# Attention before a gated layer: one transposing transfer per half tile, two V projections moved forward, weighted values in two halves

## What is computed

```
qkv = (x @ Wqkv).reshape(b, l, 3, H, DH)          # H = 16 heads of DH = 16
q = q * cos + rotate_half(q) * sin ; k likewise
scores = einsum('bqhd,bkhd->bhqk', q, k) * DH ** -0.5
out = einsum('bhqk,bkhd->bqhd', softmax(scores), v)
```

## Time and profile before

| | |
|---|---|
| median of 3 runs | 1267.89 us (1267.33 to 1268.97) |
| profiled execution | 1267.04 us, its span 1265.2 us |
| attention stage | from 0 to about 546 us |
| TensorE busy | 1175.9 us (93%) |
| VectorE busy | 944.3 us (75%) |
| ScalarE busy | 897.1 us (71%) |
| GpSimd busy | 580.8 us (46%) |
| DMA moved | 194.50 MB, mean 154 GB/s |

### The profile page before, as it was taken

How to read it: one execution, slowest core, us unless ns; L and a number is a source line. 1 busy time by engine, 2 the same in 40 slices (tenths; PEclk the granted TensorE clock), 3 DMA queues, 4 the chain that set the end, 5 groups by cost and what they waited for, 6 DMA issues and landing times. The chain is left out here.

```text
span 1265.2 us, 25878 instructions
## 1 busy us (share of the span) xinstructions
PE 1175.9 (93%) x8369; PEld 863.4 (68%) x8416; DVE 944.3 (75%) x1865; ACT 897.1 (71%) x1979; POOL 580.8 (46%) x593
## 2 busy tenths in 40 slices
PE   3699999999999999879999969999999999999997
PEld 2233333333333333258899969999999999999897
DVE  4588878778888888559666657777777777777586
ACT  5277877777777776757655457777777777777686
POOL 6232323232323210026377735666666666666763
PEclk8599999999999999999799989999999999999999
DMA  6735655564644451042032267677777776776463
GB/s 152 129 72 148 131 146 127 138 129 92 138 86 100 83 115 35 18 159 68 1 132 92 98 194 246 235 256 255 236 234 240 255 249 236 234 247 204 140 196 103
DMA packets 260826, 194.50 MB, mean 154 GB/s; under 512 B 152272, under 2 KB 243664, under 8 KB 260752
## 3 DMA queue, kind: packets, MB, share of 16 engines
q1 hardware_dynamic: 253936, 174.82, 49.0%
q0 software_dynamic: 6816, 18.75, 4.1%
HBM read 122.06 MB, written 37.52 MB: 126 GB/s over the span
## 5 line engine op out<-in xcount | busy, mean ns | idle before, releaser
L554 DVE TENSOR_REDUCE att_mx<-att_psA 128x1 f32<-128x512 f32 x512 | 330.2, 681 | 90.3 <-PE att_psA L357 89.9
L462 ACT ACTIVATE att_prob<-att_psB 128x512 f32<-128x512 f32 x512 | 289.4, 604 | 116.0 <-PE att_psB L367 101.3
L357 PE MATMUL att_psA<-att_qk 96*128 96x512 bf16 x512 | 198.9, 393 | 17.2 <-DVE att_mx L554 7.2
L1642 ACT ACTIVATE exp_psU<-exp_psU,ew_b 128x256 f32<-128x256 f32 x312 | 126.9, 446 | 102.6 <-PE exp_psU L1599 102.6
L367 PE MATMUL att_psB<-att_qk 128*128 128x512 bf16 x465 | 176.8, 383 | 9.6 <-DMA att_qk<-att_mrow 8.2
L1693 DVE CAST exp_hh<-exp_psU 128x512 fp32r<-128x512 f32 x156 | 107.8, 691 | 102.8 <-ACT exp_psU L1642 102.8
L1582 PE MATMUL exp_psD<-exp_w2h,exp_hh 128*128 128x256 f32 x624 | 175.7, 282 | 0.0
L1597 PE MATMUL exp_psU<-exp_xh,exp_w1h 128*128 128x256 f32 x624 | 173.5, 278 | 1.4 <-DVE exp_xl L1684 1.4
L1599 PE MATMUL exp_psU<-exp_xh,exp_w1l 128*128 128x256 f32 x624 | 173.0, 277 | 0.0
L1598 PE MATMUL exp_psU<-exp_xl,exp_w1h 128*128 128x256 f32 x624 | 173.0, 277 | 0.0
L1583 PE MATMUL exp_psD<-exp_w2l,exp_hh 128*128 128x256 f32 x624 | 172.4, 276 | 0.0
(11 more groups left out here) (228 smaller groups left out, 2860.4 us busy)
## 6 DMA issues: line engine op xcount, KB each, us to landing
ew_w<-ew SPq DMA_DIRECT2D x40, 1024.0 KB, 5.7
exp_w<-ew SPq DMA_DIRECT2D x38, 1024.0 KB, 6.3
slots_x<-pre_acc SPq DMA_DIRECT2D x13, 780.0 KB, 4.7
pre_spare<-slots_x SPq DMA_DIRECT2D x39, 260.0 KB, 4.1
out_g<-rows_y SPq DMA_DIRECT2D x32, 256.0 KB, 3.8
ew_b<-eb SPq DMA_DIRECT2D x39, 128.0 KB
pre_spare<-xT SPq DMA_DIRECT2D x8, 512.0 KB, 5.2
attn_rows<-att_ob SPq DMA_DIRECT2D x8, 512.0 KB, 2.8
```

What stands on the lines that cost most here:

```text
L357: pe.matmul(psA[A_BANK[n % U]][:, :], r[:, 0, qt * P:(qt + 1) * P], r[:, 1, :], start=True, stop=True).then_inc(s_amm, 1)
L462: act.activation(prob[:, n % PR, :], psB[B_BANK[n % U]][:, :], ACT.Exp, scale=SCALE).then_inc(s_exp, 1)
L554: dve.reduce_max(mx[:, g % 2, n % U:n % U + 1], psA[A_BANK[n % U]][:, :], AX_X).then_inc(s_max, 1)
```

## The change

- The stack of a tile is laid out by head, q and k side by side (`[P, 2, H, 2, P]`), and so is `qk`. One transposing transfer takes both of a half tile; it waits for both. Semaphore counts go from 32 to 16 a tile. The rotation's and the pieces' access patterns follow.
- V of tiles 2 and 3 (`LATE_ASIDE`) is projected at the end of period -3 into psB[2] and psV, before the scores begin. The waits on psX no longer ask for V in periods up to 0; instead the first row score waits for 2 copies of V, the first column score for 3.
- Weighted values are added in two halves of the 512 queries, at units 2 and 3 of each four. The output copy goes from unit 3 to 4, its turn from 6 to 5.
- The maxima are turned by four matmuls, one for each row tile, into 12 x 512 rather than by one into 48 x 128; they are copied at unit 10 instead of 11, and a transfer reads 4 rows of 512 instead of 16 of 128.
- The second repeat of pieces goes from units 10, 11 to 11, 12; the slots are zeroed with at most one transfer a period, over more periods.

```diff
+    LATE_ASIDE = (2, 3)
-    PROJECT_QK, ROPE, COPY_OUT, TURN_OUT, NORM_OUT = 0, (1, 2, 2), 3, 6, (6, 7)
-    PROJECT_V, COPY_V, SPLIT_MAX, TURN_MAX, COPY_MAX = 13, 13, 8, 10, 11
-    PIECE_1, SPREAD_1, PIECE_2, SPREAD_2, SPLIT_X = 6, (7, 8), 9, (10, 11), 0
+    PROJECT_QK, ROPE, COPY_OUT, TURN_OUT, NORM_OUT = 0, (1, 2, 2), 4, 5, (6, 7)
+    PROJECT_V, COPY_V, SPLIT_MAX, TURN_MAX, COPY_MAX = 13, 13, 8, 10, 10
+    PIECE_1, SPREAD_1, PIECE_2, SPREAD_2, SPLIT_X = 6, (7, 8), 9, (11, 12), 0
-    ADD_PV = 2
+    ADD_PV = (2, 3)
...
-        stack = a.sb("stack", [P, 2, 2, H, P], BF16)
-        qk = a.sb("qk", [P, 2, 2, H, L], BF16)
+        stack = a.sb("stack", [P, 2, H, 2, P], BF16)
+        qk = a.sb("qk", [P, 2, H, 2, L], BF16)
-        mstk = a.sb("mstk", [P, PIECES, U], BF16)
-        mrow = a.sb("mrow", [PIECES * U, 2, P], BF16)
+        mstk = a.sb("mstk", [P, PIECES, G, NT], BF16)
+        mrow = a.sb("mrow", [PIECES * G, 2, L], BF16)
-        ASIDE_QK, ASIDE_V = {1: psA[0], 2: psB[0], 3: psB[1]}, {0: psA[1], 1: psA[2]}
+        ASIDE_QK, ASIDE_V = {1: psA[0], 2: psB[0], 3: psB[1]}, {0: psA[1], 1: psA[2], 2: psB[2], 3: psV}
...
-            CLEAR = [p for p in range(NG) for _ in range((1, 1, 2, 0)[p % NT])][1:CHUNKS + 1]
+            CLEAR = [p for p in range(1, NG) if p % NT < NT - 1][:CHUNKS]
...
-                    sp.dma_start(qk[96 + k:97 + k, g // HG % 2, 0, heads(g), :].rearrange("o j (t c) -> o (j t) c", c=P),
-                                 mrow[k * U:(k + 1) * U, g % 2, :]).then_inc(s_mld[g % 2], 16)
+                    sp.dma_start(qk[96 + k:97 + k, g // HG % 2, heads(g), 0, :], mrow[k * G:(k + 1) * G, g % 2, :]).then_inc(s_mld[g % 2], 16)
...
-                for i, ready in enumerate((s_p3, s_qsp)):
-                    sp.wait_ge(s_stk, 2 * tile + 2)
-                    sp.wait_ge(ready, tile + 1)
-                    sp.dma_start_transpose(qk[:, b % 2, i, some, t * P:(t + 1) * P],
-                                           stack_of(tile)[:, i, some, :].rearrange("p h c -> p (h c)")).then_inc(s_tr[half][tile % 2], 16)
+                sp.wait_ge(s_stk, 2 * tile + 2)
+                sp.wait_ge(s_p3, tile + 1)
+                sp.wait_ge(s_qsp, tile + 1)
+                sp.dma_start_transpose(qk[:, b % 2, some, :, t * P:(t + 1) * P].rearrange("p h i c -> p (h i) c"),
+                                       stack_of(tile)[:, some, :, :].rearrange("p h i c -> p (h i c)")).then_inc(s_tr[half][tile % 2], 16)
...
                 if n == 0:
                     pe.wait_ge(s_init, SET_UP)
+                    pe.wait_ge(s_vev, 2)
...
+                if n == 0:
+                    pe.wait_ge(s_vev, 3)
...
-                for s, n in ((s_vev, p + V_LEAD), (s_qrd, p + QK_LEAD + (use > QK)),
+                for s, n in ((s_vev, p + V_LEAD if p > 0 else 0), (s_qrd, p + QK_LEAD + (use > QK)),
...
-                pe.matmul(psX[0:PIECES * U, 0:P], mstk[:, :, :].rearrange("p m u -> p (m u)"), ident[:, :], start=True, stop=True).then_inc(s_mtr, 1)
+                for t in range(NT):
+                    ins = pe.matmul(psX[0:PIECES * G, t * P:(t + 1) * P], mstk[:, :, :, t], ident[:, :], start=True, stop=True)
+                ins.then_inc(s_mtr, 1)
...
-                    m = pe.matmul(psV[32 * j:32 * j + 32, :], V[:, b % 2, kt, hg * G + j, :], prob[:, (n + j) % PR, :],
-                                  start=(kt == 0), stop=(kt == NT - 1))
-                m.then_inc(s_pv, 1)
+                    m = pe.matmul(psV[32 * j:32 * j + 32, some], V[:, b % 2, kt, hg * G + j, :], prob[:, (n + j) % PR, some],
+                                  start=(kt == 0 and part == 0), stop=(kt == NT - 1), skip_group_check=True)
+                if part == 1:
+                    m.then_inc(s_pv, 1)
...
-                    if u % G == ADD_PV and valid(n - ADD_PV - G, NG * U):
-                        add_pv((n - ADD_PV - G) // U, ((n - ADD_PV - G) % U) // G)
+                    for part in range(2):
+                        first = n - ADD_PV[part] - G
+                        if u % G == ADD_PV[part] and valid(first, NG * U):
+                            add_pv(first // U, first % U // G, part)
...
-                    if u == PROJECT_V and valid(p + V_LEAD, NT * B):
+                    if u == PROJECT_V and valid(p + V_LEAD, NT * B) and p + V_LEAD not in LATE_ASIDE:
                         project(p + V_LEAD, True)
+                if p + QK_LEAD == FILL - 1:
+                    for tile in LATE_ASIDE:
+                        project(tile, True)
```

More of the change, by code:

```diff
@@ L186, in heads_of, with by_kind @@
         def heads_of(t):
-            return t[:, :].rearrange("p (h d) -> p h d", d=DH)
+            return t[:, :].rearrange("p (h i d) -> p h i d", i=2, d=DH)
+        def by_kind(t):
+            return t[:, :].rearrange("p (h i d) -> p i h d", i=2, d=DH)
         def stack_of(tile):
@@ L192, in stack_of, with by_unit @@
                 some = prob[:, PR // 2 * (tile - 2):PR // 2 * (tile - 1), :].rearrange("p n l -> p (n l)").bitcast(BF16)
-                return some.rearrange("p (i h c) -> p i h c", i=2, h=H)
+                return some.rearrange("p (h i c) -> p h i c", i=2, h=H)
             return stack[:, tile % 2]
         def terms(tile):
-            return stack_of(tile).rearrange("p i h (m d) -> p (i h) m d", d=DH)
+            return stack_of(tile).rearrange("p h i (m d) -> p h i m d", d=DH)
+        def by_unit(t):
+            return t.rearrange("p j t -> p (j t)")
         def heads(g):
@@ L302, in _ @@
                 put(pool.memset(stack_of(tile)[:, :, :, KR:], 0.0))
-                put(pool.memset(stack_of(tile)[:, 1, :, KR:KR + PIECES], 1.0))
+                put(pool.memset(stack_of(tile)[:, :, 1, KR:KR + PIECES], 1.0))
             assert done[0] == PADDED
@@ L351, in score_rows @@
                     pe.wait_ge(s_init, SET_UP)
+                    pe.wait_ge(s_vev, 2)
                 if n % (2 * U) == 0:
                     for k in range(2):
-                        wait(pe, s_tr[half][k], 32 * NT // 2 * (b + 1))
+                        wait(pe, s_tr[half][k], 16 * NT // 2 * (b + 1))
                 wait(pe, s_max, n - last_use(A_BANK, n) + 1)
-                r = qk[0:KR, b % 2, :, h % H]
+                r = qk[0:KR, b % 2, h % H]
                 pe.matmul(psA[A_BANK[n % U]][:, :], r[:, 0, qt * P:(qt + 1) * P], r[:, 1, :], start=True, stop=True).then_inc(s_amm, 1)
@@ L385, in turn_max, with add_pv @@
                 wait(pe, s_msp, g + 1)
-                pe.matmul(psX[0:PIECES * U, 0:P], mstk[:, :, :].rearrange("p m u -> p (m u)"), ident[:, :], start=True, stop=True).then_inc(s_mtr, 1)
-            def add_pv(g, kt):
+                for t in range(NT):
+                    ins = pe.matmul(psX[0:PIECES * G, t * P:(t + 1) * P], mstk[:, :, :, t], ident[:, :], start=True, stop=True)
+                ins.then_inc(s_mtr, 1)
+            def add_pv(g, kt, part):
                 b, hg = g // HG, g % HG
-                if kt == 0:
+                some = slice(part * L // 2, (part + 1) * L // 2)
+                if kt == 0 and part == 0:
                     wait(pe, s_oev, g)
@@ L410, in project @@
                 b, t = tile // NT, tile % NT
-                bank = aside(tile, value) or psX
+                bank = psX if aside(tile, value) is None else aside(tile, value)
                 if bank is psX and tile > 0:
@@ L458, in exps @@
                     for k in range(2):
-                        act.wait_ge(s_tr[1][k], 32 * NT // 2)
+                        act.wait_ge(s_tr[1][k], 16 * NT // 2)
                 if n % G == 0:
@@ L481, in piece_1 @@
                     for half in range(2):
-                        wait(act, s_tr[half][tile % 2], 32 * (tile // 2))
-                act.activation(terms(tile)[:, :, 0, :], heads_of(rr), ACT.Copy).then_inc(s_p1, 1)
+                        wait(act, s_tr[half][tile % 2], 16 * (tile // 2))
+                act.activation(terms(tile)[:, :, :, 0, :], heads_of(rr), ACT.Copy).then_inc(s_p1, 1)
             def piece_2(tile):
                 wait(act, s_r1, tile + 1)
-                act.activation(terms(tile)[:, :, 4, :], heads_of(r1), ACT.Copy).then_inc(s_p2, 1)
+                act.activation(terms(tile)[:, :, :, 4, :], heads_of(r1), ACT.Copy).then_inc(s_p2, 1)
             def repeat_1(tile, i):
-                st = stack_of(tile)[:, i].rearrange("p h (m d) -> p h m d", d=DH)
+                st = terms(tile)[:, :, i]
                 wait(act, s_p1, tile + 1)
@@ L576, in copy_max @@
                 wait(dve, s_mld[g % 2], 16 * PIECES * (g // 2))
-                dve.tensor_copy(mrow[:, g % 2, :], psX[0:PIECES * U, 0:P]).then_inc(s_mev, 1)
+                dve.tensor_copy(mrow[:, g % 2, :], psX[0:PIECES * G, :]).then_inc(s_mev, 1)
             def norm_out(g, k):
@@ L596, in rope @@
                 b, t = tile // NT, tile % NT
-                x, half = heads_of(aside(tile, False) or psX), DH // 2
```

(9 more changed lines are left out.)

18 lines of the change are left out of this document (9 added, 9 removed).

## The result

The changed kernel takes 1280.39 us (median of 4 runs, 1278.85 to 1282.23) against 1268.43 us for the kernel before (1267.33 to 1270.35): the ratio is 1.0093, with a 95% interval of 1.0071 to 1.0115. It is 12 us slower, where 1280.5 us and slower were forecast. The profiled execution took 1278.85 us, its span 1277.0.

A forecast was written before the change was run, and what follows sets the result against it. TensorE's work plus its waits bounds the attention loop (15.42 us a period). +0.75 a period gives +23.9, single waits -3.9, start -6.5: +13.5 on 1267.0 is 1280.5 us; range 1272 to 1288, down to 1258 with the no-wait rival.

The forecast's parts named there:

- the moved wait: TensorE's output turn waits on ScalarE: score 4, exponential 4, output copy, 1.51 us against 0.87: +0.65 us a period.
- the maxima's turn: Four matmuls instead of one turn the row maxima on TensorE: +0.17 to +0.37, taken as +0.27 us a period.
- The blocks: Each weighted-values block cut into halves pays a second changeover on TensorE: +0.24 us a block, +0.95 a period.
- Rival C: Between a half block and the scores: second changeover is free, 30 us less, 1251 us; chance 0.10.
- Rival B: At the output's turn: ScalarE has copied in time, no wait, 20 us less, 1260 us; chance 0.12.
- rival D: At the maxima's turn: another wait, for VectorE's split maxima, if its chain is 0.3 us later; +9, 1289 us; chance 0.10.
- The waits that go: TensorE's waits at row scores 6 and 9, V and first column score (0.33, 0.29, 0.38, 0.12) vanish: -1.12 us a period.
- Single waits: Occasional long TensorE waits for the maxima's transfer, shortened by 0.7 us more lead: -2.4, and -1.5 later, total -3.9 us.
- The end: Late attention stage: five periods without QK projection +3.7 us, last ones +0.7, waits at 520.97 and later -1.5.
- The start: Before the first column score: V of tiles 2 and 3 projected earlier brings it forward, -6.5 us (bounds -5 to -7.5).
- The merged transposes: SyncE's transposing transfers: one merged transfer takes 2.7 us, so merging gains nothing (bounds 0.5 lost, 2 gained).
- shared fixed part: At the start: by the skill's coalescing rule, merged transfers share a fixed cost and gain some 2 us more, sum +11.5.

The follow-up runs named there:

- Two experiments: Changed kernel with the output's turn moved to unit 6: 1261.93 us, 0.9942; changed kernel with the output copy moved to unit 3: 1253.67 us, 0.9904.

## Why the prediction was right

- **The bound.** TensorE's own work and its waits made up the period before and after, and their changes add up: 0.93 + 0.36 + 0.77 - 1.12, less 0.03 for the turn and 0.10 for V, is 0.81, as measured; +0.75 was forecast. Misses inside the period cancel in part: 0.12 and 0.09 too little for the moved wait and the maxima's turn, 0.13 too much for V and the output's turn.
- **The blocks.** Forecast +0.24 each, measured +0.23, and the halves side by side show that it is paid per block and not per matmul. Rival C fell: a second changeover is not free.
- **The moved wait.** The chain of 1.51 us came out to the hundredth; the wait was 0.77 instead of 0.65, since 0.15 pass between the end of the copy and the first turning matmul. Two experiments remove the wait from either side and get 0.60 and 0.77 us a period back. Rival B fell.
- **The maxima's turn.** The term was mis-sized and split otherwise: the matmuls cost 0.15 more, under the lower bound of 0.17, and a wait of 0.21 for the split came with them. The sum had nothing for that wait. It is rival D, which had a chance of 0.10, at two thirds of its size: some 6 of the 12 us.
- **The waits that go.** All four are gone, as forecast. That 0.10 more came at V, which takes 0.72 instead of 0.82 when it follows a score directly, was not foreseen.
- **Single waits.** -2.4 forecast in the loop, about -5.0 measured. The step that failed is the cause: 0.7 us more lead was to shorten them, but the coarser transfer removes them with no more lead at all.
- **The end.** +2.9 forecast, +4.9 measured. The periods without QK projection grew by 1.1 us, not 0.75: before, they had fewer waits to lose (0.9 us, 13.8 against 12.9 of work, in place of 1.12).
- **The start.** -6.5 forecast, -6.4 measured at the first column score, but this is luck: without the late weights the same start gives -7.6, just outside the bounds. The moved projections alone give 6.9 of it. The merged transposes, priced at nothing, bring the first column score 0.7 forward; in the time this cannot be told. The 2 us more that the forecast named for a shared fixed part did not show.

The sum was +13.5 on 1267.0; the medians show +12.0. Part of the closeness is luck: the term for single waits was 2.6 too small and the end 2.0 too small, of opposite sign; the late weights hid 1.3 of the start; and the stages behind the attention took 2.6 less in the profiled execution.

## What to carry to other kernels

Where an engine's queue is the bound, price a change as its work plus each wait in order, by start to start of its instructions; a block cut in two to fill another engine's gaps costs a second changeover of the array (0.23 us here), and moving two of that engine's operations behind the one that is waited for took away one of the waits (0.33 us) at no cost. When a producer and its reader both move by a unit, walk the chain from the last shared event on each side: a unit (0.44 us) of order cost 0.6 us a period, 19 us in all. After each wait that is taken away, look for the next one on the same chain before counting the gain.

## What was not expected of the hardware

- Transfers of 4 KB into one partition as 16 rows of 256 bytes landed up to 3.6 us after their issue instead of 1.7, and TensorE waited up to 1.9 us for them; with 4 rows of 1 KB such waits never came in eight profiles.
- One such wait, of 1.89 us, was followed by a granted clock of 0.50 for three microseconds, which cost another 1.6 us; shorter ones were not.
- A block of fp32 matmuls in four column groups takes 1.00 us from its start to the next instruction, whether it is 4 matmuls of 512 columns or 8 of 256.
- Four bf16 matmuls of 128 columns with 12 columns of weights take 0.32 us, 0.08 each, against 0.12 for the fp32 turns with 128 columns of weights.
